# A router that normalises its rows once, in a ring of three buffers, and scatters second choices a step later

## The chip, the cores and the metric
The kernel runs on one core of one Trainium2 chip. The metric is the device time of one execution in microseconds (us), lower is better. Three runs of the kernel before gave 1625.89, 1629.61 and 1629.79 us, median 1629.61.

## The reference, cut to what matters
64 sequences of 128 rows of 128 numbers go through four stages with residuals: an attention layer with 16 heads over 128 + 120 keys, a mixture of experts, a second attention layer, and adapters. The change is in the first layer's end, where the rows are routed to the experts:

```python
x = x + attention0(layernorm(x), side, ctx)            # 16 heads of 8, 248 keys
xn = layernorm(x)
mixed = xn @ wqkv.T; q, k, v = split(mixed, 3)         # 8 numbers each
logits = einsum(softmax(q[..., :, None] * k[..., None, :]), v)
top_logits, idx = top_k(logits, 2)
scores = softmax(top_logits)
for e in range(8): h = silu(a) * g @ w2[e].T           # a, g = split(xn @ w1[e].T, 2)
x = x + sum over the two choices of score * h of the chosen expert
```

So each of the 8192 rows goes to two experts, with two gates that add up to one.

## The kernel before, in words
Sequences are taken in 16 groups of four (`NG`, `GB`). The first attention layer is one software pipeline over steps -4 to 17. In step g TensorE computes the scores of group g, the row maxima of group g+1 from the same stacks, and small jobs for other groups. A step has 8 units (u = 0 to 7) with numbered places, and the order on each engine is written out by hand: `jobs` gives TensorE's jobs as (unit, place, name), `ROUTE_STAGES` gives VectorE's router stages, which run behind the row maxima of a place (u, k), each with the number of groups that it is behind g.

Every engine runs its instructions in order and waits on semaphores.

Keys and queries are split into three bf16 parts on GpSimd (`split`, L406 to L412), written to HBM by SyncE (`write_k` L321, `write_q` L326), and read back in another layout as stacks (`load_k` L331, `load_q` L337). In step g that is done for group g+2. Each group's stacks come in two halves; the first half is what the first row-maxima matmul of step g+1 needs (L851). SyncE's order in a step: context loads of group g+3 (they wait for `v_ctx_ready`, the context copy of GpSimd at L453), `write_k`, store of the last result, `write_q`, `load_k(0)`, `load_q(0)`, x and source loads, and, when all scores of step g are done, `load_k(1)`, `load_q(1)`.

The router (`class Router`) works on the output of the layer one group behind: `statistics` on VectorE, `deviation` and `normalise` on GpSimd, transposes on TensorE (job RX at unit 6, L1181, which waits for `R_normed`), then logits, the two best experts, and slots (two groups behind). Normalised rows stand in `R_xn`, one buffer for even and one for odd groups, and within it one copy of the rows for the first and one for the second choice, for behind the 128 numbers of a row stands its gate. `form_slots` (L1124, L1125) writes both gates. `scatter` (L1213) sends rows of both copies with four indirect DMAs each to the slots of their experts in HBM.

GpSimd's order in step g, before: key split of g+2; the layer's deviation for g+3 (L446, L448); context copy of g+1 (L453); query split of g+2; first scatter of g-3; bias add of g (L469); router's deviation and first normalisation of g-1 (L1205 to L1041); second scatter of g-3; normalisation of g+3 (L481); second normalisation of g-1. In step 16 VectorE does both normalisations of group 15, and the remaining scatters follow in steps 16 and 17. Behind the layer, all engines meet, and the expert tiles begin.

Of the kernel before, what the change touches and what calls it, by code (L numbers as in the profile page):

```python
# [9 lines left out]
ALU = mybir.AluOpType  # L10
# [74 lines left out]
def attention_layer(nc, x_in, x_out, side_t_in, ctx_in, ctx_t_in, layer, consts, route, stacks, ys=None, expert_w=None):  # L85
# [84 lines left out]
    with ExitStack() as c:  # L170
# [229 lines left out]
        def _(pool):  # L400
# [32 lines left out]
            def step(g):  # L433
# [82 lines left out]
            if first:  # L516
                for p in range(2):
                    nc.gpsimd.memset(rt.xn[p][:, :, :, D:ROW], 0.0)
                fill_rest(0)
                pool.wait_ge(route.consts_loaded, 48)  # L520
# [90 lines left out]
        def _(dve):  # L611
# [131 lines left out]
            def between(g, u, k):  # L743

                if (u, k) in INPUT_STAGES and (g + 3).exists:
                    stage, part = INPUT_STAGES[u, k]
                    stage(g + 3, part)
                if first and (u, k) in ROUTE_STAGES:
                    behind, stage, part = ROUTE_STAGES[u, k]
                    if (g + -behind).exists:  # L750
                        stage(rt, dve, g + -behind, part)

            def step(g):
                g1 = g + 1
# [205 lines left out]
ROW = D + 4  # L960
TILES = TOKENS * TOP // S + E - 1
# [18 lines left out]
class Router:  # L980
# [5 lines left out]
    def __init__(self, nc, c, route, sem, out_t, passed, emptied):  # L986
# [5 lines left out]
        self.xn = two(lambda p: sb(f"xn{p}", [S, TOP, GB, ROW]))  # L992
# [11 lines left out]
        self.slot = two(lambda p: sb(f"slot{p}", [S, GB, TOP], mybir.dt.uint32))  # L1004
        (self.stats_ready, self.aggregated, self.eps_added, self.rstd_ready, self.normed, self.shifted, self.exp_ready,
         self.gap_ready, self.e2_ready, self.hits_ready, self.slot_ready, self.order, self.copied) = (sem("R_" + n) for n in (
             "stats_ready", "aggregated", "eps_added", "rstd_ready", "normed", "shifted", "exp_ready", "gap_ready",
             "e2_ready", "hits_ready", "slot_ready", "order", "copied"))
        self.scattered = two(lambda p: two(lambda k: sem(f"R_scattered{p}{k}")))
# [12 lines left out]
    def statistics(self, dve, g, part):  # L1022
# [3 lines left out]
        if part < 2:  # L1026
            for b in range(2 * part, 2 * part + 2):
                self.nc.vector.bn_stats(self.stats[:, b], self.out_t[g.par][:, b]).then_inc(self.stats_ready, 1)
        else:
            wait_apart(dve, self.stats_ready, (g.n + 1) * GB, self.passed)  # L1030
            wait(dve, self.copied, g.n)
            for b in range(GB):
                last = self.nc.vector.bn_aggr(self.mv[:, b], self.stats[:, b])
            last.then_inc(self.aggregated, 1)

    def normalise(self, eng, vec, g, k):
        eng.wait_ge(self.rstd_ready, g.n + 1)

        wait(eng, self.scattered[g.par][k], g.pair * GB * 16)
        for b in range(GB):  # L1040
            last = vec.tensor_scalar(self.xn[g.par][:, k, b, 0:D], self.out_t[g.par][:, b], self.mv[:, b, 0:1],  # L1041
                                     self.rstd[:, b:b + 1], ALU.subtract, ALU.mult)
        last.then_inc(self.copied if k else self.normed, 1)
# [61 lines left out]
    def form_slots(self, dve, g, part):  # L1105
# [16 lines left out]
        else:  # L1122
            self.after(dve, g, "slots")
            v.tensor_copy(self.xn[g.par][:, 0, :, D], self.g0[:])  # L1124
            v.tensor_tensor(self.xn[g.par][:, 1, :, D], self.e2[:], self.g0[:], ALU.mult)  # L1125
            v.tensor_copy(self.slot[g.par][:], self.slot_f[:]).then_inc(self.slot_ready, 1)
# [49 lines left out]
    def fill(self, pe, g, name, misc):  # L1176
        mm = self.nc.tensor.matmul
        if name == "RX":
            pe.wait_ge(self.normed, g.n + 1)
            for b in range(GB):  # L1180
                last = self.nc.tensor.transpose(misc[:, b * S:(b + 1) * S], self.xn[g.par][:, 0, b, 0:D], self.route.ident[:])  # L1181
# [20 lines left out]
    def deviation(self, pool, g):  # L1202
        wait(pool, self.copied, g.n)
# [5 lines left out]
    def scatter(self, pool, g, k):  # L1209
        pool.wait_ge(self.slot_ready, g.n + 1)  # L1210
        pool.wait_ge(self.copied, g.n + 1)
        for b in range(GB):
            self.nc.gpsimd.indirect_dma_start(  # L1213
                out=self.route.xs, out_offset=bass.IndirectOffsetOnAxis(ap=self.slot[g.par][:, b, k:k + 1], axis=0),
                in_=self.xn[g.par][:, k, b], in_offset=None).then_inc(self.scattered[g.par][k], 16)

    def scattering_done(self, pool):
        for p in range(2):
            for k in range(TOP):
                pool.wait_ge(self.scattered[p][k], NG // 2 * GB * 16)  # L1220
# [6 lines left out]
    (1, 2): (2, Router.form_logits, 1), (2, 0): (2, Router.form_logits, 2), (2, 2): (2, Router.pick, 0),  # L1227
# [513 lines left out]
```

## Time and profile before

| | |
|---|---|
| median of the runs | 1629.61 us |
| span of the profiled execution | 1619.5 us |
| what lies around the span (median less span) | 10.1 us |
| TensorE busy | 1352.2 us (83%) |
| VectorE busy | 1128.8 us (70%) |
| GpSimd busy | 984.3 us (61%) |
| ScalarE busy | 873.4 us (54%) |
| first layer, roughly | 0 to 686 us of the span |

The page gives no total for the profiled execution itself, only its span. Engines are PE (TensorE; PEld its weight loads), DVE (VectorE), ACT (ScalarE), POOL (GpSimd) and SP (SyncE; SPq its DMA issues). L12 is line 12 of the kernel. Tiles stand as output<-inputs. An idle time and what ended it stand in brackets behind an instruction. A granted clock of 1.00 is TensorE at 2.4 GHz, 0.5 is 1.2 GHz.

### The profile page before, as it was taken

The page shows a single profiled execution, that of the slowest core. Times are in us where ns is not written, and L with a number is a line of the kernel's source. Part 1 is how long each engine was busy: PE and PEld are TensorE (multiplying, and loading weights), DVE is VectorE, ACT ScalarE, POOL GpSimd, SP SyncE. Part 2 cuts the span into 40 slices and gives each one's busy share as a digit, 9 for nine tenths or more (in the row PEclk, how much of TensorE's full clock was granted, in tenths as well). Part 3 has the DMA queues.
Part 4 walks back from the last instruction along what each step waited for, and adds up shares of the span by engine and source line. Part 5 has one row for each costly group of instructions (what it writes and reads, how often), then busy time and mean ns, then how long its engine had stood idle before and what let it go on. Part 6 is the DMA issues. An engine that isn't in the chain of part 4 may idle for free. (4 is left out here: it accounts for less than half of the span.)

```text
span 1619.5 us, 46602 instructions
## 1 busy us (share of the span) xinstructions
PE 1352.2 (83%) x16805; PEld 1116.4 (69%) x16805; DVE 1128.8 (70%) x3395; ACT 873.4 (54%) x1634; POOL 984.3 (61%) x1122
## 2 busy tenths in 40 slices
PE   1689899898999988199999992369898889959999
PEld 0368677777777777199999991157676767747777
DVE  5779877787888885456555553368887888647776
ACT  1267666666766657066666660145565566624444
POOL 4447678777788866544444444888888886012221
PEclk9799999899999999599999995689999999969999
DMA  6667766666666642322222223678888787221221
GB/s 179 191 185 230 211 202 184 181 184 184 210 192 181 212 133 86 122 62 66 65 65 64 64 63 91 162 186 218 219 223 229 218 219 220 77 65 66 78 71 53
DMA packets 197816, 239.32 MB, mean 148 GB/s; under 512 B 39281, under 2 KB 165105, under 8 KB 190433
## 3 DMA queue, kind: packets, MB, share of 16 engines
q1 hardware_dynamic: 164608, 209.51, 42.5%
q0 software_dynamic: 26848, 25.91, 7.6%
q8 instruction: 131, 2.15, 0.6%
q10 hardware_dynamic: 6144, 1.06, 0.4%
q14 instruction: 85, 0.69, 0.1%
HBM read 148.34 MB, written 87.00 MB: 145 GB/s over the span
## 5 line engine op out<-in xcount | busy, mean ns | idle before, releaser
L701 DVE TENSOR_REDUCE L_neg_max<-L_ps_mx 128x2 f32<-128x496 f32 (+1 forms) x768 | 492.1, 659 | 140.0 <-PE L_ps_mx L851 136.5
L580 ACT ACTIVATE L_p<-L_ps_sc 120x512 f32<-120x512 f32 (+1 forms) x768 | 419.3, 598 | 228.3 <-PE L_ps_sc L838 225.7
L851 PE MATMUL L_ps_mx<-stack_k,stack_q 118*128 118x248 bf16 (+1 forms) x2048 | 303.3, 252 | 53.2 <-DMA stack_q<-L_q_rows 27.7
L838 PE MATMUL L_ps_sc<-stack_q,stack_k 122*120 122x128 bf16 (+1 forms) x3072 | 303.0, 223 | 6.1 <-DMA stack_q<-L_mT 4.7
L838 PEld LDWEIGHTS L_ps_sc<-stack_q,stack_k 122*120 122x120 bf16 (+1 forms) x3072 | 243.8, 124 | 69.0 <-issue 39.9
L428 POOL DMA_INDIRECT L_x<-routed_out,route_slots_all x128 | 200.9, 1570 | 49.0 <-issue 31.5
L871 PE MATMUL L_ps_o<-L_p,L_v 120*9 120x128 f32 (+1 forms) x6144 | 225.5, 281 | 3.3 <-ACT L_o_sb L607 2.7
L851 PEld LDWEIGHTS L_ps_mx<-stack_k,stack_q 118*128 118x128 bf16 x2048 | 149.7, 101 | 102.5 <-DVE L_neg_max L701 42.1
L871 PEld LDWEIGHTS L_ps_o<-L_p,L_v 120*9 120x9 f32 (+1 forms) x6144 | 145.8, 92 | 43.2 <-issue 25.3
L1436 DVE TENSOR_TENSOR M_hT<-M_act_a,M_ps_g 128x384 f32<-128x384 f32 x135 | 74.8, 554 | 126.3 <-ACT M_act_a L1396 120.4
L1344 POOL COPY M_w<-stack_q 128x384 f32 x135 | 69.1, 512 | 144.2 <-PE M_ps_y L1377 138.0
L1213 POOL DMA_INDIRECT routed_in<-R_xn,R_slot x128 | 127.0, 993 | 40.4 <-issue 32.2
L1391 ACT COPY M_w<-stack_k 128x768 f32 x135 | 112.1, 832 | 55.9 <-PE M_ps_g L1368 36.6
L1368 PE MATMUL M_ps_a<-M_xT,M_w 128*128 128x128 f32 x810 | 113.3, 276 | 0.0
L1368 PE MATMUL M_ps_g<-M_xT,M_w 128*128 128x128 f32 x810 | 113.1, 276 | 0.0
L1377 PE MATMUL M_ps_y<-M_w,M_hT 128*128 128x128 f32 x810 | 112.6, 275 | 0.0
L406 POOL TENSOR_TENSOR L_rem<-L_kf,L_k_parts_sb 128x512 f32<-128x512 f32 (+1 forms) x30 | 42.2, 1406 | 112.9 <-ACT L_k_parts_sb L545 94.1
L1396 ACT ACTIVATE M_act_a<-M_ps_a 128x384 f32<-128x384 f32 x135 | 66.2, 490 | 73.1 <-PE M_ps_a L1368 73.1
L1041 POOL TENSOR_SCALAR R_xn<-L_out,R_mv,R_rstd 128x128 f32<-128x128 f32 x120 | 94.2, 792 | 18.3 <-DMA routed_in<-R_xn,R_slot 17.8
L1368 PEld LDWEIGHTS M_ps_g<-M_xT,M_w 128*128 128x128 f32 x810 | 101.9, 193 | 0.0
L1368 PEld LDWEIGHTS M_ps_a<-M_xT,M_w 128*128 128x128 f32 x810 | 101.7, 193 | 0.3 <-DVE M_xT L1430 0.3
L1377 PEld LDWEIGHTS M_ps_y<-M_w,M_hT 128*128 128x128 f32 x810 | 101.3, 192 | 0.2 <-DVE M_hT L1436 0.2
(193 smaller groups left out, 2432.1 us busy)
## 6 DMA issues: line engine op xcount, KB each, us to landing
L_q_rows<-L_q_parts_sb SPq DMA_DIRECT2D x192, 192.0 KB
stack_q<-L_q_rows SPq DMA_DIRECT2D x192, 192.0 KB
stack_k<-L_k_rows SPq DMA_DIRECT2D x96, 372.0 KB
stack_k<-L_k_rows SPq DMA_DIRECT2D x96, 180.0 KB
L_k_rows<-L_k_parts_sb SPq DMA_DIRECT2D x32, 372.0 KB
M_x<-routed_in SPq DMA_DIRECT2D x135, 66.0 KB, 1.8
routed_out<-M_y POOLq DMA_DIRECT2D x135, 64.0 KB
x<-L_out SPq DMA_DIRECT2D x32, 256.0 KB, 3.6
```

Of the source, the lines that this page charges most:

```text
L428: nc.gpsimd.indirect_dma_start(out=x_t[g4.n % NX][:, b], out_offset=None, in_=ys, in_offset=bass.IndirectOffsetOnAxis(ap=route.slots_all[: ...
L580: nc.scalar.activation(p_t[t][u % 2][:, quarter * 4 * S:(quarter + 1) * 4 * S], ps_sc[n % NSC][0:KEYS[t], :], ACT.Exp).then_inc(sc_read, 1)
L701: nc.vector.tensor_reduce(neg_max[:, b, kk * HPB:(kk + 1) * HPB], v, AX.X, ALU.max, negate=True).then_inc(max_read, 1)
L838: last = mm(ps_sc[n % NSC][0:KEYS[t], j * S:(j + 1) * S], k_st[p][:, b // 2, h, b % 2, k0:k0 + KEYS[t]], q_st[p][:, b // 2, h, b % 2], sta ...
L851: last = mm(ps_mx[i % NMX][:, j * NK:(j + 1) * NK], q_st[p][0:TERM_TOP, b // 2, h, b % 2], k_st[p][0:TERM_TOP, b // 2, h, b % 2], start=Tr ...
L871: last = mm(ps_o[r:r + DH + 1, col:col + S], v_t[t][p][:, b, h, :], p_t[t][u % 2][:, j * S:(j + 1) * S], start=(t == 0), stop=(t == NT - 1))
L1041: last = vec.tensor_scalar(self.xn[g.par][:, k, b, 0:D], self.out_t[g.par][:, b], self.mv[:, b, 0:1], self.rstd[:, b:b + 1], ALU.subtract, ...
L1213: self.nc.gpsimd.indirect_dma_start(out=self.route.xs, out_offset=bass.IndirectOffsetOnAxis(ap=self.slot[g.par][:, b, k:k + 1], axis=0), i ...
L1368: last = nc.tensor.matmul(out[:, k * S:(k + 1) * S], w1[th % NW][:, half + k * 128:half + (k + 1) * 128], xT[p][:], start=True, stop=True)
L1377: last = nc.tensor.matmul(ps_y[p][:, 0:D], hT[p][:, k * S:(k + 1) * S], w2[ty % NW][:, k * D:(k + 1) * D], start=(k == 0), stop=(k == FC - 1))
L1391: nc.scalar.copy(w1[tw % NW][:], w1_all[:, bass.ds(e_w * W1, W1)]).then_inc(w1_ready, 1)
L1436: nc.vector.tensor_tensor(hT[p][:], act_a[p][:], ps_g[p][:, 0:FC * S], ALU.mult).then_inc(hT_ready, 1)
```

## The change: what it does
- `R_xn` becomes a ring of three buffers, each with one copy of the rows. A group's rows are normalised once, in buffer n % 3. Group 15 alone has a second copy, in another buffer of the ring.
- The first scatter of a group goes as before, in step n+3. The second goes one step later, in step n+4, at the head of GpSimd's step, from the same rows: `regate` on VectorE overwrites the gate column with the second gate (kept in `second`), at place (1,1) behind the layer's last statistics stage, once the first scatter has landed.
- GpSimd's order in step g is now: second scatter of g-4; key split; layer's deviation; context copy; query split; router's deviation and normalisation of g-1; first scatter of g-3; normalisation of g+3; bias add of g.
- In steps 16 and 17 (`NG`, `NG + 1`) the remaining scatters are placed anew: first of 13 and of 14 in step 16, second of 13 and 14 and both of 15 in step 17. VectorE normalises group 15 once in step 16, and a second time in step 17.
- Slots are kept in a ring of three too, and waits on `copied` become waits on `normed`.

```diff
@@ gpsimd, step(g)
                 if first:
+                    if (g + -4).exists:
+                        rt.scatter(pool, g + -4, 1)
                     if later:
                         wait_apart(pool, q_split, g2.n, passed)
...
                         split([qf[:]], q_parts, q_split, (g2.n - 1) * 4 + (2 if KP_FIRST else 0))
-                    late = g.n < NG
+                    if (g + -1).exists:
+                        rt.deviation(pool, g + -1)
+                        if g.n < NG:
+                            rt.normalise(pool, nc.gpsimd, g + -1, 0)
                     if g.n <= NG and (g + -3).exists:
                         rt.scatter(pool, g + -3, 0)
-                    if g.n == NG:
-                        rt.scatter(pool, g + -3, 1)
-                    if g.exists:
-
-                        pool.wait_ge(normed, g.n + 1)
-                        r = x_t[g.n % NX]
-                        nc.gpsimd.tensor_tensor(r[:], r[:], bo_bc[:].unsqueeze(1).to_broadcast([S, GB, D]),
-                                                ALU.add).then_inc(res_ready, 1)
-                    if (g + -1).exists:
-                        rt.deviation(pool, g + -1)
-                    if (g + -1).exists and late:
-                        rt.normalise(pool, nc.gpsimd, g + -1, 0)
-                    if late and (g + -3).exists:
-                        rt.scatter(pool, g + -3, 1)
...
                         last.then_inc(normed, 1)
-                    if (g + -2).exists and g.n >= NG:
+                    if g.exists:
+
+                        pool.wait_ge(normed, g.n + 1)
+                        r = x_t[g.n % NX]
+                        nc.gpsimd.tensor_tensor(r[:], r[:], bo_bc[:].unsqueeze(1).to_broadcast([S, GB, D]),
+                                                ALU.add).then_inc(res_ready, 1)
+                    if g.n == NG:
+                        rt.scatter(pool, g + -2, 0)
+                    if g.n == NG + 1:
+                        rt.scatter(pool, g + -3, 1)
                         for k in range(TOP):
                             rt.scatter(pool, g + -2, k)
-                    if (g + -1).exists and late:
-                        rt.normalise(pool, nc.gpsimd, g + -1, 1)
@@ vector
+                if first and (g.n, u, k) == (NG + 1, 2, 1):
+                    rt.regate(dve, g + -3, 0)
+                if first and (g.n, u, k) == (NG + 1, 5, 3):
+                    rt.normalise(dve, nc.vector, g + -2, 1)
...
                     if first and (g.n, u) == (NG, 4):
-                        for k in range(TOP):
-                            rt.normalise(dve, nc.vector, g + -1, k)
+                        rt.normalise(dve, nc.vector, g + -1, 0)
@@ class Router
+    def regate(self, dve, g, part):
+
+        i = self.rows(g, 0)
+        dve.wait_ge(self.scattered[i][0], self.scatters_of(i, 0, g.n + 1))
+        self.nc.vector.tensor_copy(self.xn[i][:, :, D:D + GATE_COLUMNS], self.second[g.par][:]).then_inc(self.regated, 1)
...
     def scatter(self, pool, g, k):
         pool.wait_ge(self.slot_ready, g.n + 1)
-        pool.wait_ge(self.copied, g.n + 1)
+        pool.wait_ge(self.normed, g.n + 1)
+        if k and g.n == NG - 1:
+            pool.wait_ge(self.copied, 1)
+        elif k:
+            pool.wait_ge(self.regated, g.n + 1)
+        i = self.rows(g, k)
...
 ROUTE_STAGES = {
-    (1, 2): (2, Router.form_logits, 1), (2, 0): (2, Router.form_logits, 2), (2, 2): (2, Router.pick, 0),
+    (1, 1): (4, Router.regate, 0), (1, 2): (2, Router.form_logits, 1), (2, 0): (2, Router.form_logits, 2), (2, 2): (2, Router.pick, 0),
```

`normalise` waits until the second scatter that used its buffer before has landed, `rows(g, k)` gives the buffer and `scatters_of` the count to wait for.

## Rows read from the trace of the kernel before

**Rows 1.** Waits of PE, 170 to 600 us: us in total, times, longest.
```profile
PE L_misc L1181 <- POOL R_xn L1041: 33.0, 11, 4.5
...
PE L_ps_mx L851 <- DMA stack_q<-L_q_rows: 0.2, 1, 0.2
```
**Rows 2.** Timeline of PE, step 9: start, us, what, [idle before <-releaser].
```profile
403.28 0.37 PE L851 MATMUL L_ps_mx<-stack_k,stack_q 118*128 118x248 bf16 x2 [0.30 <-DVE L_neg_max L701]
...
431.33 0.63 PE L1181 MATMUL L_misc<-C_ident,R_xn 128*128 128x128 f32 x4 [2.74 <-POOL R_xn L1041]
...
438.67 0.37 PE L851 MATMUL L_ps_mx<-stack_k,stack_q 118*128 118x248 bf16 x2 [0.20 <-DVE L_neg_max L701]
```
**Rows 3.** Timeline of POOL, step 9.
```profile
408.71 1.16 POOL L406 TENSOR_TENSOR L_rem<-L_kf,L_k_parts_sb 128x512 f32<-128x512 f32 x1 [4.09 <-ACT L_k_parts_sb L545]
...
416.55 1.16 POOL L406 TENSOR_TENSOR L_rem<-L_qf,L_q_parts_sb 128x512 f32<-128x512 f32 x1 [0.48 <-ACT L_q_parts_sb L540]
...
418.48 1.16 POOL L412 TENSOR_TENSOR L_q_parts_sb<-L_rem,L_q_parts_sb 128x512 bf16<-128x512 f32 x1
419.80 1.11 POOL L1213 DMA_INDIRECT routed_in<-R_xn,R_slot  x1 [0.17 <-issue]
...
423.76 0.95 POOL L1213 DMA_INDIRECT routed_in<-R_xn,R_slot  x1 [0.31 <-issue]
...
425.98 0.25 POOL L1205 TENSOR_SCALAR R_rstd<-R_mv 128x4 f32<-128x4 f32 x1
...
428.05 3.13 POOL L1041 TENSOR_SCALAR R_xn<-L_out,R_mv,R_rstd 128x128 f32<-128x128 f32 x4 [0.69 <-DMA routed_in<-R_xn,R_slot]
```
**Rows 4.** Timeline of SP's DMA issues, step 9.
```profile
417.03 0.91 SPq L321 DMA_DIRECT2D L_k_rows<-L_k_parts_sb  x2
...
419.66 4.92 SPq L326 DMA_DIRECT2D L_q_rows<-L_q_parts_sb  x6
```
**Rows 5.** Windows: us, busy PE, PEld, DVE, ACT, POOL, PEclk, DMA share, GB/s.
```profile
417.00:437.00 20.00, 17.10 (x304) 14.39 (x303) 15.31 (x48) 11.52 (x25) 16.83 (x19) 1.00 0.92 273
...
438.00:439.00 1.00, 0.81 (x12) 0.64 (x10) 1.00 (x2) 1.00 (x3) 1.00 (x2) 1.00 0.00 0
...
578.00:579.00 1.00, 0.81 (x10) 0.63 (x14) 0.00 (x0) 0.15 (x1) 0.82 (x2) 1.00 0.00 0
```
**Rows 6.** Query split ends and stack waits, steps 0/1, 2/3, 13; clock behind the first.
```profile
86.12 1.16 POOL L412 TENSOR_TENSOR L_q_parts_sb<-L_rem,L_q_parts_sb 128x512 bf16<-128x512 f32 x1
...
104.64 0.38 PE L851 MATMUL L_ps_mx<-stack_k,stack_q 118*128 118x248 bf16 x2 [2.22 <-DMA stack_q<-L_q_rows]
...
104.60:108.00 3.40, 3.36 (x46) 2.34 (x47) 1.26 (x2) 0.73 (x2) 0.00 (x0) 0.61 0.77 207
...
153.25 1.16 POOL L412 TENSOR_TENSOR L_q_parts_sb<-L_rem,L_q_parts_sb 128x512 bf16<-128x512 f32 x1
...
172.03 0.39 PE L851 MATMUL L_ps_mx<-stack_k,stack_q 118*128 118x248 bf16 x2 [0.23 <-DMA stack_q<-L_q_rows]
...
563.28 1.16 POOL L412 TENSOR_TENSOR L_q_parts_sb<-L_rem,L_q_parts_sb 128x512 bf16<-128x512 f32 x1
```
**Rows 7.** Timeline of PE: M of steps 4 and 14.
```profile
209.43 0.37 PE L851 MATMUL L_ps_mx<-stack_k,stack_q 118*128 118x248 bf16 x2 [0.20 <-DVE L_neg_max L701]
...
585.54 0.37 PE L851 MATMUL L_ps_mx<-stack_k,stack_q 118*128 118x248 bf16 x2 [0.20 <-DVE L_neg_max L701]
```
**Rows 8.** Timeline of DVE: last statistics stage in steps 1 and 9.
```profile
112.12 0.37 DVE L677 BATCH_NORM_AGGREGATE L_mv<-L_stats 128x2 f32<-128x6 f32 x4
...
409.90 0.36 DVE L677 BATCH_NORM_AGGREGATE L_mv<-L_stats 128x2 f32<-128x6 f32 x4
```
**Rows 9.** Timeline of DVE and POOL, end of the layer.
```profile
650.45 0.38 DVE L1033 BATCH_NORM_AGGREGATE R_mv<-R_stats 128x2 f32<-128x6 f32 x4
...
660.60 1.09 POOL L1213 DMA_INDIRECT routed_in<-R_xn,R_slot  x1 [5.14 <-DVE R_slot L1126]
...
679.78 0.96 POOL L1213 DMA_INDIRECT routed_in<-R_xn,R_slot  x1 [0.30 <-issue]
```

More of the change, by code:

```diff
@@ L516, in _ @@
             if first:
-                for p in range(2):
-                    nc.gpsimd.memset(rt.xn[p][:, :, :, D:ROW], 0.0)
+                for rows in rt.xn:
+                    nc.gpsimd.memset(rows[:, :, D:ROW], 0.0)
                 fill_rest(0)
@@ L960 @@
 ROW = D + 4
+RING = 3
+GATE_COLUMNS = 1
 TILES = TOKENS * TOP // S + E - 1
@@ L991, in __init__ @@
         self.stats, self.mv, self.rstd = sb("stats", [S, GB, 6]), sb("mv", [S, GB, 2]), sb("rstd", [S, GB])
-        self.xn = two(lambda p: sb(f"xn{p}", [S, TOP, GB, ROW]))
+        self.xn = [sb(f"xn{i}", [S, GB, ROW]) for i in range(RING)]
+        self.second = two(lambda p: sb(f"second{p}", [S, GB, 1]))
         self.xnT, self.qkv = sb("xnT", [D, GB * S]), sb("qkv", [S, GB, 3 * E])
@@ L1003, in __init__, with rows, scatters_of @@
         self.slot_f = sb("slot_f", [S, GB, TOP])
-        self.slot = two(lambda p: sb(f"slot{p}", [S, GB, TOP], mybir.dt.uint32))
+        self.slot = [sb(f"slot{i}", [S, GB, TOP], mybir.dt.uint32) for i in range(RING)]
         (self.stats_ready, self.aggregated, self.eps_added, self.rstd_ready, self.normed, self.shifted, self.exp_ready,
[L1006 to L1009, printed above, removed]
+         self.gap_ready, self.e2_ready, self.hits_ready, self.slot_ready, self.order, self.copied, self.regated) = (
+             sem("R_" + n) for n in (
+                 "stats_ready", "aggregated", "eps_added", "rstd_ready", "normed", "shifted", "exp_ready", "gap_ready",
+                 "e2_ready", "hits_ready", "slot_ready", "order", "copied", "regated"))
+        self.scattered = [two(lambda k: sem(f"R_scattered{i}{k}")) for i in range(RING)]
+    def rows(self, g, k):
+        return (g.n + 1) % RING if k and g.n == NG - 1 else g.n % RING
+    def scatters_of(self, i, k, before):
+        return sum(self.rows(Group(n // 2, n % 2), k) == i for n in range(before)) * GB * 16
     CHAIN = ("products", "max", "weighted", "reciprocals", "logits", "top", "top_index", "index", "picked",
@@ L1030, in statistics @@
             wait_apart(dve, self.stats_ready, (g.n + 1) * GB, self.passed)
-            wait(dve, self.copied, g.n)
+            wait(dve, self.normed, g.n)
             for b in range(GB):
@@ L1037, in normalise @@
         eng.wait_ge(self.rstd_ready, g.n + 1)
-        wait(eng, self.scattered[g.par][k], g.pair * GB * 16)
+        i = self.rows(g, k)
+        wait(eng, self.scattered[i][1], self.scatters_of(i, 1, g.n))
         for b in range(GB):
-            last = vec.tensor_scalar(self.xn[g.par][:, k, b, 0:D], self.out_t[g.par][:, b], self.mv[:, b, 0:1],
+            last = vec.tensor_scalar(self.xn[i][:, b, 0:D], self.out_t[g.par][:, b], self.mv[:, b, 0:1],
                                      self.rstd[:, b:b + 1], ALU.subtract, ALU.mult)
+        if k:
+            eng.wait_ge(self.slot_ready, g.n + 1)
+            last = vec.tensor_copy(self.xn[i][:, :, D:D + GATE_COLUMNS], self.second[g.par][:])
         last.then_inc(self.copied if k else self.normed, 1)
+    def regate(self, dve, g, part):
+        i = self.rows(g, 0)
+        dve.wait_ge(self.scattered[i][0], self.scatters_of(i, 0, g.n + 1))
+        self.nc.vector.tensor_copy(self.xn[i][:, :, D:D + GATE_COLUMNS], self.second[g.par][:]).then_inc(self.regated, 1)
     def form_products(self, dve, g, part):
@@ L1123, in form_slots @@
             self.after(dve, g, "slots")
-            v.tensor_copy(self.xn[g.par][:, 0, :, D], self.g0[:])
-            v.tensor_tensor(self.xn[g.par][:, 1, :, D], self.e2[:], self.g0[:], ALU.mult)
-            v.tensor_copy(self.slot[g.par][:], self.slot_f[:]).then_inc(self.slot_ready, 1)
+            second = self.second[g.par][:]
+            v.tensor_copy(self.xn[self.rows(g, 0)][:, :, D], self.g0[:])
+            v.tensor_tensor(second[:, :, 0], self.e2[:], self.g0[:], ALU.mult)
+            v.tensor_copy(self.slot[g.n % RING][:], self.slot_f[:]).then_inc(self.slot_ready, 1)
             v.tensor_copy(self.route.slots_f[:, bass.ds(g.n * (GB * TOP), GB * TOP)], self.slot_f[:].rearrange("s b k -> s (b k)"))
@@ L1180, in fill @@
             for b in range(GB):
-                last = self.nc.tensor.transpose(misc[:, b * S:(b + 1) * S], self.xn[g.par][:, 0, b, 0:D], self.route.ident[:])
+                last = self.nc.tensor.transpose(misc[:, b * S:(b + 1) * S], self.xn[self.rows(g, 0)][:, b, 0:D], self.route.ident[:])
         elif name == "RQ":
@@ L1202, in deviation @@
     def deviation(self, pool, g):
-        wait(pool, self.copied, g.n)
+        wait(pool, self.normed, g.n)
         wait_apart(pool, self.aggregated, g.n + 1, self.passed)
```

9 lines of the change are left out of this document (5 added, 4 removed).

## The prediction

> **What bounds the kernel now.** I read the waits of TensorE first: over 170 to 600 us nearly all it waits for is the router's transposes, which need GpSimd's normalised rows: 33.0 us in 11 waits; the stack of queries costs it 0.2 us [rows 1]. That looks like the thing to remove. So I followed one step (step 9) on each engine. I count from M, the step's first row-maxima matmul, the one that needs the stacks loaded in the step before: 403.28 us here, and 438.67 for the next step [rows 2]. TensorE reaches the router's transposes at M+25.3 (428.59), waits 2.74 us, and needs 7.3 us more to the next M: 35.4 us in all.
>
> On GpSimd [rows 3] the key split starts at 408.71 (M+5.4) after 4.09 us of idleness, the context copy ends at 416.07, the query split at 419.64 (M+16.4). Then come four scatter DMAs (419.80 to 424.71: 4.9 us with the gaps), the bias add, the deviation, and the four normalising instructions, which end at 431.18 (M+27.9) and release TensorE.
>
> There is a second chain, which the waits hardly show. SyncE issues the key writes at 417.03, right after the context copy for which its context loads wait, the query writes at 419.66 as the query split ends, and the loads of both stacks behind them [rows 4]. The 16 DMA engines are then 0.92 busy at 273 GB/s, and quiet only from 438 us, after the x and source loads that follow [rows 5]. The next M is at 438.67. How long this chain is can be read where TensorE waited for it: the query split ended at 87.28 and M came at 104.64 (17.4 us); 154.41 and 172.03 (17.6 us) [rows 6]. In the last such step (13), where no context, x or source is loaded any more, the engines are idle from 578 us, 13.6 us after the split's end at 564.44 [rows 5, 6]. So in an ordinary step the stacks are complete near M+16.4+17 = M+33.4. Steps 4 to 13, all that have both a key split and an old group to scatter, take 585.54 - 209.43 = 376.1 us, 37.6 us each [rows 7]. **The slack of the stack chain is 2 us in step 9 and 4 us in the mean.**
>
> **The change part by part.**
> *One normalisation instead of two.* 60 GpSimd instructions of 0.78 us go, four a step, 3.1 us, as their twins in [rows 3]. They stand at the end of GpSimd's step, ahead of 4.09 us in which it idles anyway. Their worth in steps 4 to 13 is what the next point leaves of it.
>
> *The second scatter at the head of the next step.* The four DMAs cost the same 4.9 us. But ahead of them GpSimd now waits for VectorE to rewrite the gate column, and VectorE does that behind the maxima of place (1,1), behind the last statistics instruction, which ends at 410.26 [rows 8]. A copy of 128x4 is one small instruction; four aggregates there take 0.36 us [rows 8], so its bounds are 0 and 0.36, and I take 0.16. So the scatter starts at M+7.2, not in the idle time that ends at M+5.4. Queued behind it on GpSimd stand the key split, the layer's deviation, the context copy and the query split; for them wait SyncE's context loads, key writes, query writes and all stack loads. Step by step: 7.2 + 4.9 = M+12.1 key split starts (now 5.4); 7.4 us to the end of the context copy (408.71 to 416.07, the query split's start less its idle time), M+19.5; 3.1 us of query split, whose input has been there since M+13, M+22.6 (now 16.4). **The query split ends 6.2 us later.** VectorE's wait for the first scatter costs nothing: that was issued a step before.
>
> *Deviation and normalisation ahead of the first scatter.* 1.4 + 0.1 + 3.1 us: the rows are ready at M+27.2, against 27.9. The reordering takes away 4.9 + 1.3 us and the new head gives back 6.2. TensorE's wait for the router stays at about 2 us.
>
> *Stacks.* 22.6 us and the chain behind it. The bytes are the same, they start later together. Bounds: 13.6 us (step 13) and 17.6 us. I take 17.0, near the two direct readings, since ordinary steps carry the same transfers. The next M is then at 39.6. TensorE is done at 25.3 + 2 + 7.3 = 34.6 and stands still for 5 us.
>
> *Clock.* Where M came after a wait of 2.22 us for the stacks (104.64), the granted clock was 0.61 over the next 3.4 us, a stretch partly at the lower level (1.2 GHz), and the statistics ended at 112.49, M+7.85 instead of M+7.0 [rows 6, 8]. That delays the gate copy and the whole chain. Bounds 0 and 0.85 us a step; I take 0.5, as some waits of this size leave the clock up (the one at 428.59 does: 1.00 over 417 to 437 [rows 5]). Period: 40.1 us.
> The Trainium skill (TensorE: Matmul & The Clock Gate, What's actually happening) says that a throttled clock is the default and activity releases it, so a wait for the stacks in every step would be paid twice. The row at 104.64 agrees. By it in every step the sum would be 3 us longer.
>
> *Step 13.* Its chain has fewer transfers: 22.6 + 14 = 36.6 us.
> *Step 3.* No second scatter yet at its head (that starts with group 0 in step 4), and the reordering works as drawn: from 172.03 TensorE needs 25.3 + 7.3 = 32.6, and the stacks land near 188.3 + 17 = 205.3 (its query split, like that of step 9, about M+16.3). So M at about 205.4 instead of 209.43: 4.0 us gained.
> *Steps 14 on.* No splits; nothing of GpSimd's binds until the end.
> *End of the layer.* Now VectorE normalises group 15 twice in a row ahead of the slots of 14, which release GpSimd at 660.60 after 5.14 us, and 16 scatters run to 680.74, 1.28 us from one to the next [rows 9]. After: the second scatter of group 12 goes ahead (behind the gate copy at its place (1,1), some 7 us before the statistics, so it ends near 649), the deviation no longer stands behind eight scatters but waits for the statistics alone, which end at 650.83 [rows 9], so it is done at 652.2; then 24 DMAs without a gap (13, 14 first choice; 13, 14 second; 15 both), 652.3 + 23 x 1.28 + 0.96 = 682.7. The gate rewrite of group 14 has to wait for its first scatter and has 5 us to do so. +2.0 us; bounds 0 and +5 (four scatters more behind the slots).
>
> *Sum.* Steps 4 to 12: 9 x 40.1 = 360.9; step 13: 36.6; together 397.5 against 376.1: +21.4. Step 3: -4.0. End: +2.0. In all +19.4. Span 1619.5 becomes 1638.9. Around the span lie 10.1 us (the median of the runs shown, 1629.6, less the span; the page gives no other total for its own execution), which the change doesn't touch: **1649 us**. The later layers run the same work.
>
> The Trainium skill (DMA: Bandwidth & Descriptors, Where 436 GB/s comes from) puts the limit for a core's HBM traffic near 358 GB/s. The stretch 417 to 437 runs at 273 GB/s. If the same 5.5 MB went at the page's limit, an estimate, 15.3 us would do and the forecast would turn into a small gain; nothing in this change makes transfers faster, and I give it no chance of its own beyond the first rival.
>
> **The rivals.**
> *1. The stack chain is elastic (faster).* Its place is SyncE's queue between query split and M; the price turns at 37.6 - 22.6 = 15.0 us. If it takes 13.6 us everywhere, as in step 13, M is at 36.7 with TensorE's own 34.6 to 36 just under it: 10 x 36.5 - 376.1 = -11; with -4.0 and +2.0 a span 13 us shorter, 1616. For: with late issue SyncE finds every source ready, and one scatter less competes. Against: both direct readings are 17.4 and 17.6, and the DMA engines are 0.92 busy.
> *2. The router wait is what counts (much faster).* The scatter would have to vanish in the idle time before the key split. Then rows at M+21, no wait, period 33.4: 10 x 4.2 = 42 us, with the rest 44 us less, 1586. Against: the statistics end at M+7.0 in VectorE's order, 1.6 us behind the present start of the key split, so nothing of the scatter fits ahead of it. Only if the gate copy came far earlier.
> *3. The clock feeds on the stall (slower still).* The full 0.85 us, and 17.6 for the chain: 22.6 + 17.6 + 0.85 = 41.1; 9 x 41.1 + 37.4 - 376.1 = +31; in all +29, 1659. For: the wait would be 5 us, longer than any now in these steps. Against: the low stretch is short.
> *4. It cancels (no change).* A chain of 15 us: steps give 0, the ends -2, 1628.
>
> **How the numbers follow.** Forecast 0.62, rival 3 0.18, rival 1 0.08, rival 2 0.03, rival 4 0.09. What a measurement tells from no change is 0.3%, 4.9 us. Slower 0.80, same 0.09, faster 0.11. The range reaches from rival 4 to somewhat over rival 3: 1628 to 1666; the part left out is rivals 1 and 2 and a little above.
>
> **What would show it.** In a middle step: the key split starts 12 us after M, not 5.4; the gate copy just behind the last statistics; the key writes near M+20.5. TensorE waits 3 to 6 us for the stack of queries in nine steps, where it now waits for nothing, and still 1 to 3 us for the router's rows. The period is 39 to 41 us; step 3 is near 33.5. GpSimd's normalising instructions are 60 fewer. The forecast is wrong if the stack wait stays under 1 us, or if M to the key split is under 8 us.

## The result and the profile after

The changed kernel takes 1667.4 us (median of 4 runs, 1661.0 to 1672.8) against 1629.15 us (4 runs, 1625.9 to 1629.8): ratio 1.0232 [1.0198, 1.0266], 38 us slower. The forecast was 1649 us and its range ended at 1666; the sign, the place and the mechanism were right, the size was half of what came. The profiled execution took 1664.1 us with a span of 1662.4 us.

Spans grow by 42.9 us. By stretches:

| stretch | before, us | after, us | difference | forecast |
|---|---|---|---|---|
| start to M of step 4 | 209.4 | 202.1 | -7.3 | -4.0 |
| of it, step 3 | 37.4 | 33.2 | -4.2 | -4.0 |
| M of step 4 to M of step 14 | 376.1 | 412.1 | +36.0 | +21.4 |
| M of step 14 to the end of the last scatter | 95.2 | 101.0 | +5.8 | +2.0 |
| last scatter to the experts' first transpose | 7.4 | 8.2 | +0.8 | 0 |
| experts, second layer, adapters and end | 931.4 | 939.0 | +7.6 | 0 |

The last line is code that the change doesn't touch. Its second layer takes 450.4 us before and 459.4 after, the parts around it 1.4 us less; over the profiled runs below the second layer lies between 450.4 and 467.7 us for the same code. So the verdicts here rest on the stretches of the first layer, which moved by 35.3 us in all, and the medians beside them.

The waits of TensorE over 200 to 640 us of the kernel after (total us, times, longest):
```profile
PE L_ps_mx L852 <- DMA stack_q<-L_q_rows: 30.5, 10, 4.7
PE L_ps_mx L852 <- DVE L_neg_max L699: 27.9, 24, 2.1
```
The two lines of [rows 1] have changed places. The stack of queries, which cost 0.2 us, is now waited for in every step, and the router's rows are not in the list. Step 9 on TensorE, which answers to [rows 2], shows the same:
```profile
408.53 0.60 PE L852 MATMUL L_ps_mx<-stack_k,stack_q 118*128 118x248 bf16 x2 [3.68 <-DMA stack_q<-L_q_rows]
...
439.53 0.61 PE L1204 MATMUL L_misc<-C_ident,R_xn 128*128 128x128 f32 x4
...
449.28 0.44 PE L852 MATMUL L_ps_mx<-stack_k,stack_q 118*128 118x248 bf16 x2 [2.62 <-DMA stack_q<-L_q_rows]
```
M is 408.53, the next is 449.28: a period of 40.8 us, and the transposes of the router, reached at M+31.0, have no bracket. The statistics end and the gate copy on VectorE (answering to [rows 8]) and then GpSimd and SyncE (to [rows 3] and [rows 4]):
```profile
416.57 0.36 DVE L675 BATCH_NORM_AGGREGATE L_mv<-L_stats 128x2 f32<-128x6 f32 x4
416.85 0.14 DVE L1065 COPY R_xn<-R_second 128x4 f32<-128x4 f32 x1
```
```profile
417.80 1.07 POOL L1241 DMA_INDIRECT routed_in<-R_xn,R_slot  x1 [12.60 <-DVE R_xn L1065]
...
421.70 0.96 POOL L1241 DMA_INDIRECT routed_in<-R_xn,R_slot  x1 [0.30 <-issue]
422.69 1.17 POOL L406 TENSOR_TENSOR L_rem<-L_kf,L_k_parts_sb 128x512 f32<-128x512 f32 x1
...
431.92 1.20 POOL L412 TENSOR_TENSOR L_q_parts_sb<-L_rem,L_q_parts_sb 128x512 bf16<-128x512 f32 x1
...
434.56 3.13 POOL L1054 TENSOR_SCALAR R_xn<-L_out,R_mv,R_rstd 128x128 f32<-128x128 f32 x4
```
```profile
431.00 0.91 SPq L321 DMA_DIRECT2D L_k_rows<-L_k_parts_sb  x2
433.15 4.72 SPq L326 DMA_DIRECT2D L_q_rows<-L_q_parts_sb  x6
```
GpSimd stands idle for 12.60 us, then scatters, and only at M+14.2 does it take up the key split (M+5.4 before). The query split ends at M+24.6 (before 16.4), the query writes go out at once, and the stacks land 16.2 us later, at M+40.8. Over the nine full steps (4 to 12) the means are: key split M+14.2, query split's end M+24.6, next M at +41.5. The two transfer lines of [rows 5] and of the clock in [rows 6] have these answers (us, busy PE, PEld, DVE, ACT, POOL, granted clock, DMA share, GB/s):
```profile
408.50:412.00 3.50, 3.47 (x44) 2.29 (x45) 1.67 (x3) 0.90 (x2) 0.00 (x0) 0.51 0.77 214
...
430.00:450.00 20.00, 17.15 (x261) 14.49 (x260) 16.22 (x47) 11.37 (x23) 15.84 (x19) 0.93 0.88 275
```
The transfer rate is that of before (273 GB/s); the clock behind M, 0.51, is the lower level (1.2 GHz). M of steps 4 and 14, which answer to [rows 7]:
```profile
202.09 0.39 PE L852 MATMUL L_ps_mx<-stack_k,stack_q 118*128 118x248 bf16 x2 [0.52 <-DMA stack_q<-L_q_rows]
...
614.21 0.37 PE L852 MATMUL L_ps_mx<-stack_k,stack_q 118*128 118x248 bf16 x2 [0.20 <-DVE L_neg_max L699]
```
And the end of the layer, to [rows 9]:
```profile
684.27 1.12 DVE L1054 TENSOR_SCALAR R_xn<-L_out,R_mv,R_rstd 128x128 f32<-128x128 f32 x4 [4.31 <-DMA routed_in<-R_xn,R_slot]
```
```profile
714.27 0.96 POOL L1241 DMA_INDIRECT routed_in<-R_xn,R_slot  x1 [0.30 <-issue]
```

### The profile page after: what moved, and what is told of

Its sections match the earlier page's. It is cut to its first block and busy times, and to the rows that moved or that the text cites. A ratio compares the mean times of both kernels' runs of the same rounds, so it can differ in the third digit from the quotient of the medians.

```text
span 1662.4 us, 46546 instructions
## 1 busy us (share of the span) xinstructions
PE 1361.8 (82%) x16805; PEld 1122.7 (68%) x16805; DVE 1157.1 (70%) x3411; ACT 875.0 (53%) x1634; POOL 936.0 (56%) x1063
## 5 line engine op out<-in xcount | busy, mean ns | idle before, releaser
L852 PE MATMUL L_ps_mx<-stack_k,stack_q 118*128 118x248 bf16 (+1 forms) x2048 | 307.0, 255 | 102.7 <-DMA stack_q<-L_q_rows 58.2
L839 PE MATMUL L_ps_sc<-stack_q,stack_k 122*120 122x128 bf16 (+1 forms) x3072 | 307.3, 225 | 4.0 <-DMA stack_q<-L_mT 2.3
L839 PEld LDWEIGHTS L_ps_sc<-stack_q,stack_k 122*120 122x120 bf16 (+1 forms) x3072 | 247.5, 126 | 67.2 <-issue 39.7
L605 ACT COPY L_o_sb<-L_ps_o 128x512 f32<-128x512 f32 x128 | 75.3, 589 | 29.8 <-DVE L_rden L648 21.2
```

The costliest lines, as they stand in the source:

```text
L605: nc.scalar.copy(o_sb[:], ps_o[:]).then_inc(o_read, 1)
L839: last = mm(ps_sc[n % NSC][0:KEYS[t], j * S:(j + 1) * S], k_st[p][:, b // 2, h, b % 2, k0:k0 + KEYS[t]], q_st[p][:, b // 2, h, b % 2], sta ...
L852: last = mm(ps_mx[i % NMX][:, j * NK:(j + 1) * NK], q_st[p][0:TERM_TOP, b // 2, h, b % 2], k_st[p][0:TERM_TOP, b // 2, h, b % 2], start=Tr ...
```

## The experiments

Theory A, that of the prediction with its sizes mended: the second scatter at the head of GpSimd's queue holds back the splits until the gate copy is there, and the stacks' chain of some 17 us behind the query split sets M. Rival B: with one copy of the rows the router's normalisation or the ring of buffers is what costs. Rival C: VectorE's casts of the router, which became 14 times longer (below), carry the loss. The recorded expectations speak of Theory S, which is A, and of Theory V, by which the loss sits on VectorE and TensorE themselves (gate copies, casts held up, low clock); C is its part that can be tested alone. "Steps" is the time from M of step 4 to M of step 14, 376.1 us before and 412.1 after; times of TensorE's place count from M.

| kernel | median, us | ratio to before | steps, us | M of step 14 to last scatter, us |
|---|---|---|---|---|
| late_ring4 | 1600.3 | 0.9824 [0.9780, 0.9868] | 338.1 | 106.2 |
| late_ring3 | 1654.1 | 1.0130 [1.0072, 1.0189] | 395.0 | 100.5 |
| gate_early | 1599.3 | 0.9817 [0.9773, 0.9861] | 348.0 | 97.6 |
| gate_later | 1707.1 | 1.0465 [1.0412, 1.0518] | 448.1 | 105.0 |
| pick_early | 1660.6 | 1.0197 [1.0130, 1.0264] | 413.3 | 99.9 |
| scatter_first | 1673.8 | 1.0256 [1.0202, 1.0309] | 415.2 | 102.2 |
| one_norm | 1627.5 | 0.9984 [0.9958, 1.0010] | 377.8 | 92.9 |
| late_ring4_end | 1597.5 | 0.9813 [0.9766, 0.9861] | 338.6 | 101.4 |
| ring4_head | 1668.1 | 1.0249 [1.0176, 1.0321] | 409.5 | 98.2 |
| late_gate | 1588.9 | 0.9768 [0.9695, 0.9841] | 334.0 | 102.6 |

**late_ring4.** All of the change stays but the place of the second scatter, which goes behind the first; a fourth buffer lets the next normalisation start without waiting for it.
```
-                    if (g + -4).exists:
-                        rt.scatter(pool, g + -4, 1)
 ...
                     rt.scatter(pool, g + -3, 0)
+                    if (g + -4).exists:
+                        rt.scatter(pool, g + -4, 1)
-RING = 3
+RING = 4
```


> The changed kernel, with the second scatter of group g-4 taken from the head of GpSimd's step and put behind the first scatter of g-3, and a ring of four buffers so that this is possible. Theory S (the stack chain: gate copy, second scatter, splits, query writes, stack loads decides each step): the key split is back at M+5.4, the stacks land near M+33.3, the router's rows are ready at M+21, ahead of TensorE; steps 4 to 13 take 33.5 to 34.5 us each (41.2 in the changed kernel, 37.6 in the one before), about 1590 us. Theory V (the loss sits on VectorE and TensorE themselves: gate copies, casts held up behind GpSimd, low clock): TensorE's own step stays 4 to 5 us longer, 37 to 39 us a step, 1620 to 1640 us.

Measured: 1600.3 us, 1.8% under before, 67 us under after; the steps take 338.1 us, 74.0 less than after's, with the same DMAs and, but for the clearing of the fourth buffer, the same instructions. The key split starts at M+5.4 in each step, the query split ends at M+17.4, TensorE waits for the stacks 0.4 us at most at M, and nowhere for the router. The steps are as expected (33.8 us each); the total lies above the 1590 us expected, in part because the end of the layer takes 106.2 us, 5.2 more than after's. The place of four DMAs in one in-order queue is worth all of the loss and turns it into a gain.

**late_ring3.** The ring stays at three, the second scatter stands behind the query split and ahead of the deviation.
```
-                    if (g + -4).exists:
-                        rt.scatter(pool, g + -4, 1)
 ...                                    # behind the query split
+                    if (g + -4).exists:
+                        rt.scatter(pool, g + -4, 1)
                     if (g + -1).exists:
                         rt.deviation(pool, g + -1)
```


> The changed kernel with three buffers, the second scatter of g-4 moved only behind the query split, ahead of the router's deviation, so that the normalisation into the same buffer has to wait for its landing. Theory S: stacks land near M+33 again, the router's rows at about M+28 as in the kernel before, a wait of some 3 us for them; 36 to 38 us a step, 1615 to 1632 us. Theory V: 40 us a step, above 1645 us.

Measured: 1654.1 us; 1615 to 1632 had been expected, a miss. Its step of M = 403.2 on GpSimd:
```profile
428.39 3.13 POOL L1054 TENSOR_SCALAR R_xn<-L_out,R_mv,R_rstd 128x128 f32<-128x128 f32 x4 [1.32 <-DMA routed_in<-R_xn,R_slot]
```
and the waits of TensorE over 203 to 540 us:
```profile
PE L_misc L1204 <- POOL R_xn L1054: 24.4, 8, 3.7
```
The query split ends at M+17.4 and the stacks have 4 to 8 us of slack, so the first chain is gone as A says. But the normalisation waits for a scatter just issued from the same buffer, the rows are ready at M+28.4, and TensorE, there at M+26.4, waits 2 to 4 us (5 in step 13); after that the granted clock is at the lower level for 3 to 10 us, here in all ten steps, in before in seven of them. That is the chain of before again [rows 1, 2]. I had reckoned with its wait at before's price; the steps take 39.5 us instead of before's 37.6. Beside late_ring4 it shows what the fourth buffer is for.

**gate_early** and **gate_later.** Only the place of the gate copy in VectorE's order is moved, to the step's head or one unit on.
```
-    (1, 1): (4, Router.regate, 0),
+    (0, 0): (4, Router.regate, 0),     # gate_early
+    (2, 1): (4, Router.regate, 0),     # gate_later
```


> The changed kernel with the gate copy of group g-4 moved from place (1,1) to place (0,0) of VectorE's step, nothing else. Theory S: the copy comes at M+1 instead of M+8.4, so the key split starts near M+7 instead of M+14, and the stacks land 7 us earlier, near M+34.5; 34.5 to 36 us a step, 1597 to 1612 us. Theory V: the scatter stays at the head, the gate copies stay, 1640 us or more.

> The changed kernel with the gate copy at place (2,1) instead of (1,1), about 4 us later. Theory S: every one of the ten steps gets longer by the full delay, 40 us in all: 1700 to 1712 us. Theory V: VectorE and TensorE do the same work, the key split only moves away from the casts that it holds up: 1655 to 1675 us.

Step 9 of gate_early (M = 378.7), on VectorE and on GpSimd:
```profile
379.67 0.16 DVE L1065 COPY R_xn<-R_second 128x4 f32<-128x4 f32 x1
```
```profile
380.64 1.07 POOL L1241 DMA_INDIRECT routed_in<-R_xn,R_slot  x1 [3.15 <-DVE R_xn L1065]
...
385.54 1.17 POOL L406 TENSOR_TENSOR L_rem<-L_kf,L_k_parts_sb 128x512 f32<-128x512 f32 x1
```
and of gate_later (M = 427.4):
```profile
438.92 0.16 DVE L1065 COPY R_xn<-R_second 128x4 f32<-128x4 f32 x1
```
```profile
439.89 1.07 POOL L1241 DMA_INDIRECT routed_in<-R_xn,R_slot  x1 [14.83 <-DVE R_xn L1065]
...
444.78 1.17 POOL L406 TENSOR_TENSOR L_rem<-L_kf,L_k_parts_sb 128x512 f32<-128x512 f32 x1
```
Copies at M+1.0, 8.3 and 11.5 give key splits at M+6.9, 14.2 and 17.4 and mean periods of 34.8, 41.2 and 44.8 us: the period follows the copy nearly one to one (6.4 us for 7.3, 3.6 for 3.2). That is the strongest evidence for A, since each kernel has the same instructions in the same buffers. Neither B nor C makes this line. Moving one copy of 0.16 us is worth 68 us of time to one side and 40 to the other.

**pick_early.** The two halves of the router's choice move one place forward in VectorE's order, so that the casts of the indices no longer meet GpSimd's key split.
```
-    (2, 2): (2, Router.pick, 0), (2, 3): (2, Router.pick, 1),
+    (2, 1): (2, Router.pick, 0), (2, 2): (2, Router.pick, 1),
```


> The changed kernel with VectorE's two pick stages one place earlier, (2,1) and (2,2) instead of (2,2) and (2,3), so that the cast of the two best indices (2.2 us in the changed kernel, 0.16 before) no longer falls on GpSimd's key split. Theory S (only the stack chain sets the step): TensorE comes to the router 2 to 4 us earlier after M, waits for the stacks that much longer, and the time is unchanged within 0.4%: 1660 to 1674 us. Theory V (the held-up casts are part of the loss): 2 us a step less, 1640 to 1650 us.

All casts of the indices (times, shortest, median, longest in ns), in the kernel after and then in this one:
```profile
L1119 DVE CAST R_idx_f<-R_top_i x16: 161/2243/2258, 148.3 to 694.3; 128x8 f32<-128x8 uint32 x16
```
```profile
L1119 DVE CAST R_idx_f<-R_top_i x16: 154/161/334, 148.3 to 695.0; 128x8 f32<-128x8 uint32 x16
```
The casts are short again, TensorE reaches the router at M+27.1 instead of M+30.9, and the ten steps don't get shorter: 413.3 us against 412.1. What TensorE gains it waits for: 2.2 us for the router and 3.3 to 5.8 us for the stacks. C is refuted as a cause; the casts lie in time that the stack chain covers.

**scatter_first.** In the kernel after, the first scatter goes ahead of the deviation and the normalisation, so that the rows come later and TensorE waits for them, not at M.
```
+                    if g.n <= NG and (g + -3).exists:
+                        rt.scatter(pool, g + -3, 0)
                     # deviation and normalisation, and the scatter taken away behind them
```


> The changed kernel with the first scatter put back ahead of the router's deviation and normalisation; the second stays at the head. Theory S: the stack chain is untouched, the router's rows come 5 us later, at M+34, and TensorE, which gets there at M+31, now waits 3 us for them; the step ends 1 to 3 us later than the stacks, 43 to 44 us: 1680 to 1695 us. If the reordering by itself were the harm, this would be faster than the changed kernel, 1650 us or less.

TensorE, step 9, then VectorE:
```profile
411.87 0.39 PE L852 MATMUL L_ps_mx<-stack_k,stack_q 118*128 118x248 bf16 x2 [1.60 <-DMA stack_q<-L_q_rows]
...
444.86 0.63 PE L1204 MATMUL L_misc<-C_ident,R_xn 128*128 128x128 f32 x4 [3.61 <-POOL R_xn L1054]
...
453.80 0.37 PE L852 MATMUL L_ps_mx<-stack_k,stack_q 118*128 118x248 bf16 x2 [0.20 <-DVE L_neg_max L699]
```
```profile
418.38 0.36 DVE L675 BATCH_NORM_AGGREGATE L_mv<-L_stats 128x2 f32<-128x6 f32 x4
```
```profile
411.90:415.40 3.50, 3.50 (x55) 2.59 (x56) 2.67 (x5) 2.24 (x6) 0.00 (x0) 1.00 0.74 217
```
1673.8 us, where 1680 to 1695 had been expected. The wait has moved from M to the router. Behind M the clock is granted in full (1.00 against 0.51 in after), and the statistics end at M+6.9 instead of 8.4, the key split starts at M+12.7, near the M+12.1 forecast for the change. So what lengthens M to the statistics in the kernel after is the stall just ahead of M and the clock behind it (ring4_head, below, tells the two apart). It gains nothing: the 1.5 us come back as the wait for the rows. The Trainium skill (TensorE: Matmul & The Clock Gate, What's actually happening) has it that the throttled clock is the default and activity releases it; 0.51 behind a wait of 3.68 us and 1.00 behind one of 1.60 agree with it. But the length of the wait does not settle it by itself: in step 5 of ring4_head a wait of 2.75 us (M = 243.48) had 1.00 behind it, and in step 1 of late_ring4_end one of 1.76 us (M = 103.33) had 0.56.

**one_norm.** In the kernel before, the second normalisation is replaced by one copy of the rows; the rest of the order stays, two buffers, both scatters in their old place.
```
-            for b in range(GB): ...  the second copy's four tensor_scalar
+            eng.wait_ge(self.normed, g.n + 1)
+            last = vec.tensor_copy(self.xn[g.par][:, 1, :, 0:D], self.xn[g.par][:, 0, :, 0:D])
```


> The kernel before with the four instructions of the second normalisation replaced by one copy of the normalised rows; all order as before. It tells what one normalisation less is worth by itself. Theory S: it stands ahead of GpSimd's idle time at M+5.4, so nothing: 1630 us within 0.5%. Rival (GpSimd's amount of work counts): 2 us a step, 1605 us.

1627.5 us (10 runs), ratio 0.9984: no difference that can be told. The removed instructions lay ahead of GpSimd's idle time, as the prediction had put it; the steps take 377.8 us against 376.1.

**late_ring4_end.** As late_ring4, but from step 16 on the second scatter stands at the head, where no split is behind it.
```
-                    if (g + -4).exists:
+                    if (g + -4).exists and g.n >= NG:      # at the head
+                    if (g + -4).exists and g.n < NG:       # behind the first scatter
```


> The kernel with the late second scatter and four buffers, but in steps 16 and 17 the second scatter is at the head of GpSimd's step again, where GpSimd idles 6.8 us for the last statistics. Expected: the steps as with the late scatter, the end of the layer 4 to 6 us shorter: 1592 to 1597 us, the fastest of all.

The end of the layer takes 101.4 us instead of 106.2, the steps are the same (338.6). The medians, 1597.5 and 1600.3, don't separate the two: their ratios to before have intervals that overlap.

**ring4_head.** The kernel after with a fourth buffer and nothing else.
```
-RING = 3
+RING = 4
```


> The changed kernel with four buffers instead of three and nothing else: group 15's first normalisation no longer goes into the buffer whose second scatter (group 12) was issued only some us before, where VectorE now waits 4.31 us for the landing. Expected: steps 3 to 13 unchanged (41 us each), the stretch from the M of step 14 to the last scatter 3 to 5 us shorter than 101 us. 1660 to 1666 us; if that wait is covered by other work, 101 us again.

1668.1 us: no gain (after 1667.4), where 1660 to 1666 had been expected. Steps 409.5 us, 2.6 under after's; 1.8 of them lie in step 5 (39.2 us against 41.0), the one whose wait of 2.75 us left the clock at 1.00, and there the statistics ended at M+6.9. It is a single step, but it separates the two: the low clock, and not the wait, makes the statistics late. So the ring has no part worth naming in the loss of the steps (B), and its part in the end of the layer is 2.8 us, 98.2 against 101.0. The wait of 4.31 us of the kernel after is here:
```profile
679.87 1.33 DVE L1054 TENSOR_SCALAR R_xn<-L_out,R_mv,R_rstd 128x128 f32<-128x128 f32 x4 [0.99 <-POOL R_rstd L1230]
```

**late_gate.** As late_ring4_end, and the gate copy of a step moves to place (4, 1), out of the stretch in which VectorE's small instructions hold up what the query split needs.
```
-    (1, 1): (4, Router.regate, 0),
+            if first and (u, k) == ((4, 1) if g.n < NG else (1, 1)) and (g + -4).exists:
+                rt.regate(dve, g + -4, 0)
```


> The kernel with the late second scatter, four buffers and the end at the head of the steps 16 and 17, with the gate copy moved from place (1,1) to (4,1) in steps 4 to 15. There the copy had pushed the router's logits onto GpSimd's key split (0.56 us instead of 0.24), the attention rows and the query split came 1.0 us later than in the kernel before (M+17.4 against 16.4). Theory S: the query split is back at M+16.4 and the ten steps take 33.0 to 33.5 us instead of 33.9: 3 to 8 us less, 1588 to 1594 us. Rival: TensorE itself needs 33.5 us, nothing changes.

In late_ring4 and late_ring4_end the query split ends 1.0 us later than in before, since ScalarE's cast of it comes late. Beside it stands a VectorE instruction that has grown, first in late_ring4_end, then in before:
```profile
380.87 0.56 DVE L1103 TENSOR_TENSOR R_logits<-R_weighted,R_sum 128x32 f32<-128x32 f32 x1
```
```profile
410.74 0.24 DVE L1079 TENSOR_TENSOR R_logits<-R_weighted,R_sum 128x32 f32<-128x32 f32 x1
```
With the copy elsewhere the query split ends at M+16.3 again, in nine of the ten steps:
```profile
371.44 0.38 PE L856 MATMUL L_ps_mx<-stack_k,stack_q 118*128 118x248 bf16 x2
...
396.53 0.61 PE L1208 MATMUL L_misc<-C_ident,R_xn 128*128 128x128 f32 x4
...
405.03 0.39 PE L856 MATMUL L_ps_mx<-stack_k,stack_q 118*128 118x248 bf16 x2 [0.40 <-DMA stack_q<-L_q_rows]
```
```profile
376.81 1.16 POOL L406 TENSOR_TENSOR L_rem<-L_kf,L_k_parts_sb 128x512 f32<-128x512 f32 x1 [1.08 <-issue]
...
386.58 1.16 POOL L412 TENSOR_TENSOR L_q_parts_sb<-L_rem,L_q_parts_sb 128x512 bf16<-128x512 f32 x1
```
1588.9 us, the fastest: 2.3% under before, 4.7% under after. Steps of 33.4 us against 37.6, with TensorE nowhere held for more than 0.6 us at M; the stacks now have 0 to 0.5 us of slack. Whether it beats late_ring4_end by its median is open (ratios 0.9768 and 0.9813, intervals overlap); the steps take 334.0 against 338.6 us in one profile each.

## Why the prediction was right in direction and short in size

- **"The slack of the stack chain is 2 us in step 9 and 4 us in the mean": right.** It is used up and TensorE stands still for 2.0 to 4.7 us at M in nine steps of ten (0.5 in step 4). The gate copies of the two gate kernels move the period with it.
- **The gate copy just behind the last statistics, key split near M+12: right as a mechanism, short by size.** The row of statistics ends at 416.93, the copy at 416.99, the key split starts at 422.69. From statistics to the query split's end the nine steps take 16.2 us in the mean (24.62 - 8.42); the forecast had 15.6 (22.6 - 7.0). The 0.6 us are mostly the 0.8 us between the copy's end and the first DMA (416.99 to 417.80), which the sum had at nothing. In nine steps that is 5.3 us.
- **"Clock ... I take 0.5, bounds 0 and 0.85": the step that failed.** M to the end of the statistics is 8.42 us in the mean of steps 4 to 12, not the 7.0 of before: 1.4 us, above the upper bound of the forecast. 0.92 x 9 = 8.3 us more than the sum. scatter_first takes the stall at M away and has 6.9 again. The bound came from a single wait, of 2.22 us in step 1 [rows 6], and from the wrong base: its M+7.85 was held against the M+7.0 of ordinary steps, but step 1 takes less than those where the clock is full. Step 1 of the kernel after, TensorE, its window, then VectorE:
```profile
103.35 0.39 PE L852 MATMUL L_ps_mx<-stack_k,stack_q 118*128 118x248 bf16 x2 [1.74 <-DMA stack_q<-L_q_rows]
```
```profile
103.35:106.85 3.50, 3.50 (x55) 2.62 (x56) 2.31 (x4) 1.91 (x5) 0.00 (x0) 1.00 0.79 217
```
```profile
109.33 0.37 DVE L675 BATCH_NORM_AGGREGATE L_mv<-L_stats 128x2 f32<-128x6 f32 x4
```
The statistics end at M+6.35. late_ring4 and late_ring4_end, which are the same code in this step, have M+6.35 behind a clock of 1.00 and M+7.89 behind one of 0.56. Read so, the row at 104.64 says 1.5 us, which is about what came. The lower bound rested on step 9, where the clock stays up behind the router's wait; that is one of only three such steps (9, 12 and 13). In before the clock falls during that wait or just behind it in seven of the ten steps and stays at the lower level for 3 to 10 us (steps 4 to 8, 10 and 11), as in step 8, where the wait of 4.49 us ends at 393.2:
```profile
392.10:398.90 6.80, 5.72 (x55) 4.45 (x55) 1.91 (x3) 2.16 (x4) 5.67 (x7) 0.50 0.56 168
```
In after it was lower behind M in all nine steps with a wait of 2 us or more. Rival 3 was this case in its clock, though its 17.6 us for the chain did not come, and its 1659 is nearest to the result, still 8 us short.
- **17.0 us from the end of the query split to M: right**, 16.9 in the mean. Rivals 1 and 4, an elastic chain or one of 15 us, are refuted for this order. In step 13 the stacks landed at M+36.3, 13.8 us behind the split (forecast 14), but there TensorE's own work ended last, at M+38.2 (router reached at M+30.9, and 7.3 us more): 1.6 us over the step's forecast of 36.6.
- **Sum of the steps:** 8.3 (clock) + 5.3 (release) - 0.6 (0.07 less of chain a step) + 1.6 (step 13) = 14.6 us, by which 36.0 exceeds 21.4. The spans grew by 23.5 us more than the forecast 19.4: these 14.6, 3.8 from the end of the layer, 8.4 from behind the last scatter, less 3.3 ahead of step 4. By the medians the excess is 19 us.
- **The router's wait "stays at about 2 us": wrong, and without effect.** Forecast: rows at M+27.2 and TensorE there at 25.3. Both moved: the rows are ready at M+29.2 (434.56 + 3.13), and TensorE arrives at M+30.9 in the mean. pick_early brings it to M+27.1: 3.8 of its 5.6 us are VectorE's held-up casts; that the rest goes with the slow clock behind M is not shown by itself. TensorE's own work then covers part of what the stack chain needs, and the wait at M is 3 us and not 5. With the casts short or long the period was the same.
- **Step 3, -4.0 us: right** (-4.2). What is over in the stretch ahead of step 4 (3.1 us more) lies in steps 0 to 2, which were the same in code but for the reordering and the second normalisation; the profiled runs have M of step 3 between 168.9 and 172.0, and I didn't take it apart.
- **End of the layer, +2.0, bounds 0 and +5: short, +5.8.** The buffer of group 15 is that of group 12 (both are 0 of three), whose second scatter had just been issued; VectorE waits 4.31 us for it ahead of the slots of 14, for which GpSimd waits. I had written of the wait of the gate rewrite and overlooked this one. ring4_head gives 2.8 us of it back, so the rest (98.2 against 95.2) agrees with the forecast to 1 us.
- **What lies around the span:** 1.7 us, not 10.1. The execution before that was profiled was some 8 us faster than its median, which leaves the forecast difference as it is.
- **"What would make it wrong": neither came** (stack wait under 1 us; key split under M+8). The observed period, 41.5, was outside of the 39 to 41 that I gave.

Rival 2, that the router's wait counts and the scatter must vanish, is what late_ring4 and gate_early then built: its 33.4 us a step is what late_gate measures, and its 1586 us lies 3 us from late_gate's 1588.9. The prediction held that nothing of the scatter fits ahead of the key split; it missed that the scatter could go behind, where a fourth buffer takes away the wait of the normalisation.

What stays open: why the second layer differs by up to 17 us between profiled runs of the same code, and which part of the 7.3 us of the start is the change's.

## What to carry to other kernels

In an in-order queue the price of an edit is the slack of all that stands behind it: an instruction with a wait goes behind the work that others need, and if that makes a buffer late, try a further buffer: here it was cheaper than the wait (1600.3 against 1654.1 us). A transfer chain that shows 0.2 us of waits can be the next bound; measure its length where it once was waited for, and subtract it from the period. Where an edit makes TensorE wait at the head of a step, count the clock that follows with it, on every engine that TensorE feeds there.

## What the runs showed of the hardware

- **Small VectorE instructions lasted as long as GpSimd's beside them.** In step 9 of the kernel after:
```profile
422.69 2.26 DVE L1119 CAST R_idx_f<-R_top_i 128x8 f32<-128x8 uint32 x1
424.99 1.08 DVE L1121 TENSOR_TENSOR R_picked<-route_iota_e,R_idx_f 128x64 f32<-128x64 f32 x1
```
The cast is 0.16 us alone, the second 0.23; here the cast begins with GpSimd's key split (422.69) and ends when its second instruction does. The Trainium skill (SBUF — State Buffer, Who interferes with whom) says that a VectorE instruction with two SBUF inputs, or a cast in a 2-port mode, can be shut out for the whole of a GpSimd instruction; the second row agrees with it. The cast was held for two of GpSimd's, 1.17 and 1.11 us, which is more than that sentence says, and whether it ran in such a mode no run shows.
- **A stall of 2 to 5 us on TensorE cost 1.4 us of VectorE's chain behind it** in the mean, through the clock behind it (0.50 to 0.69 over the 3.5 us from M in steps 5 to 13). Where the clock stayed at 1.00 behind a stall of 2.75 us (ring4_head, step 5), nothing was lost.
- **From the release by VectorE to the first indirect DMA 0.8 us pass** (also 379.83 to 380.64 and 439.08 to 439.89); the second follows it after 1.4 us, and those behind come every 1.26 to 1.29 us for the most part, in rows of 4, 8 (363.39 to 364.67 in late_ring4) and 16.
